# In the last 24 groups of a state-space scan, one u*B product moves from VectorE to GpSimd and its decay to PSUM

## The chip, the cores and the metric

The kernel runs on one core of a Trainium2 chip. The metric is the device time of one execution in microseconds (us); lower is better. Before the change the median of three runs is 1768.24 us (1761.63 to 1771.18).

## What is computed

The input x has 8 batches of 512 tokens with 128 channels. It is normalized, and goes through two branches whose results are multiplied and added to x: a selective state-space layer (Mamba), and a mixture of experts with a silu behind it. The 24 groups that the change touches do the first, cut here to what matters:

```
u, dt, B, C       from projections and a short convolution; 256 inner channels, 64 states, 512 tokens a batch
dA                = exp(dt[t, d] * A[d, s])                       # the decay
state[t, d, s]    = state[t-1, d, s] * dA[t, d, s] + (dt*x)[t, d] * B[t, s]
y[t, d]           = sum over s of state[t, d, s] * C[t, s]
out               = x + (x + (y + D*x_ssm) * silu(z) @ Wout) * silu(experts(x))
```

For each state s and each channel there is a recurrence over 512 tokens. Its three inputs are the decay, u*B (u is dt*x), and, for the output, C.

## The kernel before

**Tiling.** The 256 inner channels are two halves (h = 0, 1) of 128 partitions; the 512 tokens of a batch lie along the free axis. One scan instruction (VectorE, tensor_tensor_scan, 128x512) does one state of one half. The 64 states of a batch are 8 groups of 8 (SG = 8). Over 8 batches there are 64 groups, u = 0 to 63. Groups 0 to 39 carry along the routed experts' matrix work ("with blocks"); groups 40 to 63 (batches 5 to 7) don't, and instead gather the experts' rows and finish the output of batch after batch. The last group of each batch is followed by one that opens the next (40, 48, 56), with extra matrix work and extra VectorE operations (gate_y, add_xn).

**Who does what in a group**, for states i = 0 to 7:

- ScalarE makes the decays: exp with the state's A as scale, from dt_in to `decay` in SBUF (group_decay, L962 to L966). It runs one group ahead: the slot of (i, h) is free when the scan of (i, h) of the group before is done. It also makes diagonals of B (group_diag) and the gelu of the shared expert, once a group.
- u*B is made in one of several ways, by the letter of the state in `KIND` (L64). "D": the matrix unit (PE) broadcasts the row of B to a PSUM bank (bcast, L1462), and VectorE multiplies it twice, by u of each half (L1250), into two PSUM banks. "E": PE makes u*B itself with the diagonal of B (fill, L1473), a half at a time. "Q": the broadcast and one multiplication for the first half; for the second half GpSimd multiplies u by a row of B that a DMA has broadcast to SBUF (L724, into `u_q`), and its decay is written to the PSUM bank by ScalarE (q_decay_to_psum, L948). "P": both halves by GpSimd, both decays to PSUM. Before the change the groups without blocks are "DEDDEDEE", those with blocks "DEDDEQEP".
- VectorE scans: 16 scans a group into `states[:, i % 2]`, a buffer of two states. State i waits for the product of state i - 2 (L1252).
- GpSimd multiplies the finished state by C, both halves in one operation of 128x1024 (L710), once both scans are done. Without blocks it also issues three gathers a group, behind products 1, 4 and 7 (GATHER_AT, L692), 64 in all, so that groups 40 to 60 have all three and group 61 one; and in seven groups gate_attn (L701) behind product 7.
- PE adds the products up to y in PSUM (ysum, add_to_y, L1498), with products in a ring of four.
- SyncE issues the loads of each group (load_group, L464): half of the rows of C at a time, broadcast to all partitions (1024 KB). The first half for group u waits for products 0 to 3 of group u - 1, the second half for all products of group u - 1.

Order on each engine is the order of the program; each works through its own list and waits on semaphores. GpSimd's list for a group is:

```
for i in range(SG):
    (at i = 0 and 4: wait for the rows of C)
    wait scans of state i; product i                     # L708 to L713
    if blocks and i == 1:         u_b                    # L718
    if blocks and i == Q_AT - 2:  u_q                    # L724, Q_AT = 5
    if not blocks: gather at i = 1, 4, 7; gate_attn at i = 7
```

The three PSUM banks that rotate through the states are given by `BANKS`, which is worked out from KIND. States of kinds D and Q leave VectorE's product in the bank that held the state before.

Of the kernel before, what the change touches and what calls it, by code (L numbers as in the profile page):

```python
# [10 lines left out]
ACT = mybir.ActivationFunctionType  # L11
X_AXIS = mybir.AxisListType.X
ds = bass.ds

P = 128
# [4 lines left out]
def mamba_gated_moe(nc, x, norm_w, norm_b, Win, conv_w, conv_b, dt_w, dt_b, A_log, Dskip, Bp, Cp, Wout,  # L20
# [42 lines left out]

    KIND = ("DEDDEDEE", "DEDDEQEP")  # L64
    P_AT, Q_AT = SG - 1, KIND[1].index("Q")
    assert KIND[1].index("P") == P_AT and not set("PQ") & set(KIND[0])
    D_AT = [[i for i in range(SG) if kind[i] == "D"] for kind in KIND]
# [13 lines left out]
    col_of_b = lambda g, e: g if e == NE[1] else g * NE[1] + (E + e)  # L81
    DECAYS = (SCANS, SCANS - NH - 1)
    BROADCASTS = [sum(k in "DQ" for k in kind) for kind in KIND]
# [27 lines left out]
    with ctx:  # L111
# [195 lines left out]
        def _(sp):  # L307
# [147 lines left out]

            def load_b_row(u, g, tb):
                if not isinstance(u, int) or u:
                    sp.wait_ge(s["u_b_pooled"], u)
                    sp.wait_ge(s["u_q_pooled"], u)
                for n in range(2):  # L460
                    sp.dma_start(b_row[:, n, :], c_d[S + n * E:S + (n + 1) * E][ds(g, 1), ds(tb, L)].broadcast_to((P, L))
                                 ).then_inc(s["b_row_loaded"], 16)

            def load_group(b, g, block, block_before):  # L464
# [15 lines left out]
                if isinstance(u, int) and u == ADD_IN[-1] + 1:  # L480
                    sp.wait_ge(s["final_summed"], NB - 1)
                    load_gates(NB - 1)
                if block:
                    load_b_row(u, g, tb)
                load_c(b, g, 1, tb)
# [145 lines left out]
        def _(pool):  # L631
# [71 lines left out]
            def group(b, g, blocks, slot=None, slot_q=None):  # L703
                n = b * S + g * SG
                for i in range(SG):
# [8 lines left out]
                    if blocks and i == 1:  # L714
# [6 lines left out]
                            b_row[:, 0:1, :].broadcast_to((P, NH, L)), ALU.mult).then_inc(s["u_b_pooled"], 1)  # L721
                    if blocks and i == Q_AT - 2:

                        nc.gpsimd.tensor_tensor(u_q, u_in.rearrange("p n h t -> p (n h t)")[:, ds(slot_q, L)], b_row[:, 1, :],  # L724
                                                ALU.mult).then_inc(s["u_q_pooled"], 1)
# [19 lines left out]
        def _(act):  # L745
# [202 lines left out]
            def q_decay_to_psum(u, g, slot):  # L948

                act.sem_inc(s["q_bank_claimed"], 1)  # L950
                col = snap(g * SG + (S + Q_AT))
                nc.scalar.activation(ps[BANKS[True][Q_AT][1]][:], dflat[:, ds(slot + L, L)], ACT.Exp,
                                     scale=aflat[:, ds(col, 1)]).then_inc(s["q_decay_ready"], 1)
# [21 lines left out]
            def group(b, g, slot, head, block, block_before, last=None):  # L975
# [6 lines left out]
                for i in range(SG):  # L982
# [16 lines left out]
                    for h in range(NH):  # L999
                        if block_before and not second and (i, h) == (Q_AT - 1, 1):  # L1000
                            evict_block(u - 1)
                        act.wait_ge(s["scanned"], m0 + (2 * i + h + 1))
                        if block_before and (i, h) in ((P_AT - 2, 1), (P_AT - 1, 0)):
                            decay_to_psum(*before, 1 - h)
                        if block_before and (i, h) == (Q_AT - 1, 0):
                            q_decay_to_psum(*before)
                        if KIND[block][i] == "P" or (KIND[block][i] == "Q" and h) or (first and i == 0):
                            continue
                        group_decay(b, g, slot, i, h)
# [33 lines left out]
            for b in range(NB_BLK, NB):  # L1043
                run(b, False, b == NB_BLK)
            silu_of(NB - 1, ffn_ps[:])
            copy_result(NB - 1, hid_ps)
# [3 lines left out]
        def _(dve):  # L1050
# [182 lines left out]
            def group(b, g, slot, block, last=None, last_xn=None):  # L1233
# [3 lines left out]
                for i in range(SG):  # L1237
# [15 lines left out]
                    for h, bank in enumerate((first, second)):  # L1253
# [7 lines left out]
                        if KIND[block][i] == "Q" and h:  # L1261
# [5 lines left out]
                        dve.wait_ge(s["decay_ready"],  # L1267
                                    states_to(u, DECAYS, block, m + (0 if block and i > Q_AT else 1)))
                        if KIND[block][i] in "DQ":
# [458 lines left out]
```

## Time and profile before

| | |
|---|---|
| median of three runs | 1768.24 us |
| the profiled execution | 1764.14 us |
| its span | 1762.4 us, 43563 instructions |
| VectorE (DVE) busy | 1602.0 us, 91% |
| PE busy | 1549.5 us, 88% |
| GpSimd (POOL) busy | 1487.3 us, 84% |
| ScalarE (ACT) busy | 1402.0 us, 80% |
| the 24 groups without blocks | from 1159.4 to 1748.7 us |

The profile is of one execution. Busy shares are means over the whole span: they tell who is close to full, not who is waited for. Of use here are the timelines of single engines, in which each entry has its start, its length, the line and the operation; "xN" are N operations in a row, merged. In square brackets is the idle time of the engine ahead of the entry and what ended it.

### The profile page before, as it was taken

The numbers are of one execution on the slowest core, as the hardware profiler recorded it, in microseconds if no ns is written. First come the engines' busy times: TensorE is split into PE (matmuls) and PEld (weight loads), VectorE is DVE, ScalarE is ACT, GpSimd is POOL, SyncE is SP. The second block draws the span as 40 slices with busy tenths as digits, with TensorE's granted clock in tenths as the row PEclk, the third lists the DMA queues.
The fourth block names the chain that finished last, engine by engine and source line by source line (L and its number), as shares of the span: only waits on it lengthen the run. The fifth ranks groups of instructions, "written<-read, shape, count | busy, mean of one in ns | idle before, by whom it ended". The sixth has DMA issues, their size and how long they took to land. (4 is left out here: it accounts for less than half of the span.)

```text
span 1762.4 us, 43563 instructions
## 1 busy us (share of the span) xinstructions
PE 1549.5 (88%) x13334; PEld 799.8 (45%) x13334; DVE 1602.0 (91%) x1778; ACT 1402.0 (80%) x2641; POOL 1487.3 (84%) x757
## 2 busy tenths in 40 slices
PE   5784489999999999999999999988898988999888
PEld 5332254444444544444444444444443444444444
DVE  7888489999999999999999999999998999999987
ACT  4898478887888888887888788888888788888882
POOL 1355489998999999999999899989998899989976
PEclk8897699999999999999999999999999999999999
DMA  8767555676676875686667757666456464664633
GB/s 237 248 221 228 144 134 147 150 175 173 151 161 145 200 159 145 151 203 165 150 149 172 181 151 159 148 150 141 115 120 170 111 135 99 151 138 107 141 81 80
DMA packets 215321, 272.45 MB, mean 155 GB/s; under 512 B 27530, under 2 KB 106132, under 8 KB 215060
## 3 DMA queue, kind: packets, MB, share of 16 engines
q1 hardware_dynamic: 211124, 262.66, 61.6%
q0 software_dynamic: 4096, 8.40, 1.7%
q8 instruction: 69, 1.13, 0.3%
q14 instruction: 32, 0.26, 0.0%
HBM read 226.81 MB, written 43.93 MB: 154 GB/s over the span
## 5 line engine op out<-in xcount | busy, mean ns | idle before, releaser
L710 POOL TENSOR_TENSOR arena<-arena 128x1024 f32<-128x1024 f32 x512 | 1199.8, 2360 | 138.7 <-DVE arena L1275 114.6
L1275 DVE TENSOR_TENSOR_SCAN arena<-arena,ps 128x512 f32<-128x512 f32 x904 | 1045.2, 1204 | 91.3 <-POOL arena L710 57.2
L965 ACT ACTIVATE arena<-arena,neg_A 128x512 f32<-128x512 f32 (+1 forms) x904 | 605.5, 712 | 76.7 <-DVE arena L1275 73.9
L1498 PE MATMUL ps<-arena,ident 64*64 64x512 f32 x4096 | 557.0, 616 | 1.7 <-POOL arena L710 1.6
L1484 PE MATMUL ps<-arena 128*64 128x128 f32 x6912 | 469.4, 280 | 99.8 <-DVE arena L1275 96.9
L1484 PEld LDWEIGHTS ps<-arena 128*64 128x64 f32 x6912 | 374.1, 138 | 331.2 <-DVE arena L1275 179.7
L1250 DVE TENSOR_TENSOR ps<-arena,ps 128x512 f32<-128x512 f32 x472 | 301.3, 680 | 9.5 <-PE ps L1470 9.4
L972 ACT ACTIVATE arena<-ident,b_turned 128x128 f32<-128x128 f32 x864 | 272.9, 387 | 0.0
L1498 PEld LDWEIGHTS ps<-arena,ident 64*64 64x64 f32 x4096 | 107.6, 131 | 180.6 <-issue 173.7
L925 ACT ACTIVATE arena<-ps,arena 128x256 f32<-128x256 f32 x160 | 67.0, 470 | 118.8 <-PE ps L1568 118.8
L682 POOL DMA_INDIRECT x_rms_by_expert<-arena,slots x64 | 70.4, 1099 | 96.4 <-DMA x_rms_by_expert<-arena,slots 61.3
L1470 PEld LDWEIGHTS ps<-b_parts,pick 96*128 96x128 bf16 (+1 forms) x256 | 24.6, 96 | 249.3 <-issue 212.2
L1470 PE MATMUL ps<-b_parts,pick 96*128 96x512 bf16 x256 | 100.8, 394 | 40.2 <-DVE arena L1275 33.8
L718 POOL TENSOR_TENSOR arena<-arena 128x1024 f32<-128x1024 f32 x40 | 94.8, 2369 | 0.0
L1258 DVE TENSOR_TENSOR_SCAN arena<-ps,arena 128x512 f32<-128x512 f32 x80 | 93.1, 1205 | 0.2 <-POOL arena L710 0.2
L917 ACT ACT_TABLE_LOAD x64 | 82.1, 1283 | 13.9 <-PE ps L1547 9.2
L965 ACT ACT_TABLE_LOAD x70 | 89.8, 1283 | 1.2
L1576 PE MATMUL ps<-arena 128*128 128x128 f32 x640 | 89.8, 285 | 0.0
L1576 PEld LDWEIGHTS ps<-arena 128*128 128x128 f32 x640 | 82.7, 196 | 11.1 <-issue 10.0
L1568 PE MATMUL ps<-arena 128*128 128x256 f32 x320 | 86.5, 393 | 0.0
L1547 PE MATMUL ps<-x_rms,arena 128*128 128x512 f32 x128 | 67.9, 612 | 5.2 <-issue 4.5
L692 POOL DMA_INDIRECT arena<-routed_by_expert,slots x64 | 63.2, 987 | 9.5 <-issue 3.7
(171 smaller groups left out, 1138.2 us busy)
## 6 DMA issues: line engine op xcount, KB each, us to landing
arena<-c_scratch SPq DMA_DIRECT2D x128, 1024.0 KB
arena<-c_scratch SPq DMA_DIRECT2D x80, 256.0 KB, 6.4
arena<-w_routed_scaled SPq DMA_DIRECT2D x40, 256.0 KB
arena<-in_L_ffn_W_r_dram SPq DMA_DIRECT2D x40, 256.0 KB, 9.1
arena<-w_shared_tiles SPq DMA_DIRECT2D x128, 64.0 KB
x_rms_by_expert<-arena SPq DMA_DIRECT2D x1, 5120.0 KB, 28.1
arena<-x_rms_by_expert SPq DMA_DIRECT2D x40, 128.0 KB, 7.3
routed_by_expert<-arena SPq DMA_DIRECT2D x40, 128.0 KB, 8.8
```

The source lines that it names most:

```text
L710: nc.gpsimd.tensor_tensor(products[:, i % RING, :, :], states[:, i % 2, :, :], c_rows[:, i // CG, i % CG, :].unsqueeze(1).broadcast_to((P, ...
L718: nc.gpsimd.tensor_tensor(u_b, u_in.rearrange("p n h t -> p (n h t)")[:, ds(slot, NH * L)].rearrange("p (h t) -> p h t", h=NH), b_row[:, 0 ...
L965: nc.scalar.activation(decay[:, 2 * i + h, :], dflat[:, ds(slot + h * L, L)], ACT.Exp, scale=aflat[:, ds(col, 1)]).then_inc(s["decay_ready ...
L972: ins = nc.scalar.activation(diag_of(e)[:, c, :], ident[:], ACT.Copy, scale=bt_flat[:, ds(at + c, 1)])
L1250: vector.tensor_tensor(ps[bank][:], uflat[:, ds(slot + h * L, L)], ps[new][:], ALU.mult).then_inc(s["u_b_multiplied"], 1)
L1258: vector.tensor_tensor_scan(states[:, i % 2, h, :], ps[bank][:], u_b[:, h, :], 0.0, ALU.mult, ALU.add).then_inc(s["scanned"], 1)
L1275: vector.tensor_tensor_scan(states[:, i % 2, h, :], decay[:, m, :], ps[bank][:], 0.0, ALU.mult, ALU.add).then_inc(s["scanned"], 1)
L1470: mm(ps[bank][:], pick[:, ds(sel, 1)].broadcast_to((3 * SQ, P)), bflat[:, ds(col, L)], start=True, stop=True).then_inc(s["b_broadcast"], 1)
L1484: ins = mm(bank[HP * r:HP * r + HP, c * P:(c + 1) * P], u_turned[:, odd, c, h * P + HP * r:h * P + HP * r + HP], diag[:, c, :], start=True ...
L1498: ins = mm(y_ps[r][HP * h:HP * h + HP, :], ident[q, q], products[q, slot, h, :], start=False, stop=False, skip_group_check=True)
L1568: mm(bank[:, (RA, RB)[t % 2]], w1_block[:, t, :], x_block, start=True, stop=True, skip_group_check=True).then_inc(s["tile_made"], 1)
L1576: ins = mm(block_ps[:, k * C:(k + 1) * C], hidden_block[:, t, k * P:(k + 1) * P], w2_block[:, t, :], start=(t == 0), stop=(t == HT - 1), s ...
```

## The change

The kind of state 5 (the sixth) in the groups without blocks goes from D to Q. VectorE multiplies only for the first half of the channels; GpSimd makes u*B of the second half to SBUF, behind product 3; ScalarE writes the decay of the second half to the PSUM bank instead of to `decay` in SBUF, in the group in which it is read, not one ahead; SyncE loads the row of B for it (256 KB) once a group, which so far it did only with blocks. The plan of PSUM banks for these groups becomes that of the groups with blocks. For group 63 ScalarE writes its decay behind its last group.

```diff
-    KIND = ("DEDDEDEE", "DEDDEQEP")
+    KIND = ("DEDDEQEE", "DEDDEQEP")
...
-    DECAYS = (SCANS, SCANS - NH - 1)
+    DECAYS = (SCANS - 1, SCANS - NH - 1)
...
-            def load_b_row(u, g, tb):
+            def load_b_row(u, g, tb, block=True):
                 if not isinstance(u, int) or u:
-                    sp.wait_ge(s["u_b_pooled"], u)
+                    if block:
+                        sp.wait_ge(s["u_b_pooled"], u)
                     sp.wait_ge(s["u_q_pooled"], u)
-                for n in range(2):
+                for n in range(0 if block else 1, 2):
...
-                if block:
-                    load_b_row(u, g, tb)
+                load_b_row(u, g, tb, block)
                 load_c(b, g, 1, tb)
...
-                    if blocks and i == Q_AT - 2:
+                    if i == Q_AT - 2:
+                        if not blocks:
+                            pool.wait_ge(s["b_row_loaded"], (b * E + g) * 16 + (NBLK * 16 + 16))
+                            pool.wait_ge(s["dt_u_loaded"], b * 32 + 32)
+                            slot_q = (b % 2) * (NH * L) + L
                         nc.gpsimd.tensor_tensor(u_q, u_in.rearrange("p n h t -> p (n h t)")[:, ds(slot_q, L)], b_row[:, 1, :],
                                                 ALU.mult).then_inc(s["u_q_pooled"], 1)
...
-                        if block_before and (i, h) == (Q_AT - 1, 0):
+                        if not first and (i, h) == (Q_AT - 1, 0):
                             q_decay_to_psum(*before)
...
+            act.wait_ge(s["scanned"], NB * E * SCANS + 2 * (Q_AT - 1) + 1)
+            q_decay_to_psum(NB * E - 1, E - 1, (NB - 1) % 2 * (NH * L))
```

The rest of the diff carries the same through the counts of semaphores and asserts.

## Rows read from the trace of the kernel before

**Rows 1.** Costliest lines, 1160 to 1750 us; then busy time by engine in one group.

```profile
L1275 DVE TENSOR_TENSOR_SCAN arena<-arena,ps 128x512 f32<-128x512 f32 x384 | 441.4, 1202 | 27.4 <-POOL arena L710 14.1 <-PE ps L1484 8.3 <-ACT arena L965 3.2
...
core 0: us, PE busy (x) PEld busy (x) DVE busy (x) ACT busy (x) POOL busy (x), PEclk, DMA share, GB/s
...
1303.50:1326.90 23.40, 21.80 (x222) 11.57 (x224) 22.71 (x25) 20.59 (x37) 21.64 (x11) 1.00 0.57 105
```

**Rows 2.** Timeline of VectorE, group 46: start, length, line, operation, [idle before].

```profile
1313.75 4.54 DVE L1275 TENSOR_TENSOR_SCAN arena<-arena,ps 128x512 f32<-128x512 f32 x4
1318.22 1.26 DVE L1250 TENSOR_TENSOR ps<-arena,ps 128x512 f32<-128x512 f32 x2
1319.39 4.54 DVE L1275 TENSOR_TENSOR_SCAN arena<-arena,ps 128x512 f32<-128x512 f32 x4
1324.63 2.33 DVE L1275 TENSOR_TENSOR_SCAN arena<-arena,ps 128x512 f32<-128x512 f32 x2 [0.69 <-POOL arena L710]
1326.88 1.27 DVE L1250 TENSOR_TENSOR ps<-arena,ps 128x512 f32<-128x512 f32 x2
```

**Rows 3.** Timeline of GpSimd, the same group.

```profile
1316.22 4.67 POOL L710 TENSOR_TENSOR arena<-arena 128x1024 f32<-128x1024 f32 x2 [0.84 <-DVE arena L1275]
1321.04 0.99 POOL L692 DMA_INDIRECT arena<-routed_by_expert,slots  x1
1322.05 4.68 POOL L710 TENSOR_TENSOR arena<-arena 128x1024 f32<-128x1024 f32 x2
1327.10 2.36 POOL L710 TENSOR_TENSOR arena<-arena 128x1024 f32<-128x1024 f32 x1 [0.37 <-DVE arena L1275]
```

**Rows 4.** Timelines, group 38 (with blocks, state 5 a Q); then all of L724.

```profile
1127.66 0.67 DVE L1250 TENSOR_TENSOR ps<-arena,ps 128x512 f32<-128x512 f32 x1
1128.37 1.22 DVE L1275 TENSOR_TENSOR_SCAN arena<-arena,ps 128x512 f32<-128x512 f32 x1
...
1131.30 2.33 DVE L1275 TENSOR_TENSOR_SCAN arena<-arena,ps 128x512 f32<-128x512 f32 x2 [0.59 <-POOL arena L710]
...
1127.48 1.29 POOL L724 TENSOR_TENSOR arena<-arena 128x512 f32<-128x512 f32 x1
1128.72 4.68 POOL L710 TENSOR_TENSOR arena<-arena 128x1024 f32<-128x1024 f32 x2
...
L724 POOL TENSOR_TENSOR arena<-arena x40: 1259/1278/1297, 203.7 to 1151.1; 128x512 f32<-128x512 f32 x40
```

**Rows 5.** Timelines of GpSimd and VectorE, group 63 (no gathers).

```profile
1738.18 4.67 POOL L710 TENSOR_TENSOR arena<-arena 128x1024 f32<-128x1024 f32 x2 [1.06 <-DVE arena L1275]
1743.82 4.66 POOL L710 TENSOR_TENSOR arena<-arena 128x1024 f32<-128x1024 f32 x2 [0.96 <-DVE arena L1275]
...
1746.38 2.33 DVE L1275 TENSOR_TENSOR_SCAN arena<-arena,ps 128x512 f32<-128x512 f32 x2 [0.48 <-POOL arena L710]
```

**Rows 6.** Timelines: waits for others in groups 41, 43, 48, 49, 57, 62.

```profile
1184.50 1.29 DVE L1250 TENSOR_TENSOR ps<-arena,ps 128x512 f32<-128x512 f32 x2 [0.42 <-PE ps L1470]
...
1232.04 1.29 DVE L1250 TENSOR_TENSOR ps<-arena,ps 128x512 f32<-128x512 f32 x2 [0.21 <-PE ps L1470]
...
1360.30 2.33 DVE L1275 TENSOR_TENSOR_SCAN arena<-arena,ps 128x512 f32<-128x512 f32 x2 [5.69 <-PE ps L1484]
...
1384.07 1.29 DVE L1250 TENSOR_TENSOR ps<-arena,ps 128x512 f32<-128x512 f32 x2 [1.08 <-PE ps L1470]
...
1577.88 1.30 DVE L1250 TENSOR_TENSOR ps<-arena,ps 128x512 f32<-128x512 f32 x2 [0.75 <-PE ps L1470]
...
1689.17 1.28 ACT L933 ACTIVATE arena<-ident,gate_columns 128x128 f32<-128x128 f32 x4 [4.83 <-PE ps L1517]
...
1711.35 1.29 DVE L1250 TENSOR_TENSOR ps<-arena,ps 128x512 f32<-128x512 f32 x2 [4.74 <-PE ps L1470]
```

**Rows 7.** ScalarE's decays (to PSUM; to SBUF at state 4); landing times of L461.

```profile
L952 ACT ACTIVATE ps<-arena,neg_A x40: 666/692/693, 218.7 to 1150.9; 128x512 f32 x32, 128x512 f32<-128x512 f32 x8
...
1222.00 0.72 ACT L965 ACTIVATE arena<-arena,neg_A 128x512 f32<-128x512 f32 x1 [0.39 <-DVE arena L1275]
...
DMA to landing us min/median/max: 3.8/6.4/10.8
```

More of the change, by code:

```diff
@@ L58, in mamba_gated_moe @@
     N_SUM = SG
-    KIND = ("DEDDEDEE", "DEDDEQEP")
+    KIND = ("DEDDEQEE", "DEDDEQEP")
     P_AT, Q_AT = SG - 1, KIND[1].index("Q")
-    assert KIND[1].index("P") == P_AT and not set("PQ") & set(KIND[0])
+    assert KIND[1].index("P") == P_AT and "P" not in KIND[0] and KIND[0].index("Q") == Q_AT
     D_AT = [[i for i in range(SG) if kind[i] == "D"] for kind in KIND]
@@ L951, in q_decay_to_psum @@
                 col = snap(g * SG + (S + Q_AT))
-                nc.scalar.activation(ps[BANKS[True][Q_AT][1]][:], dflat[:, ds(slot + L, L)], ACT.Exp,
+                nc.scalar.activation(ps[BANKS[0][Q_AT][1]][:], dflat[:, ds(slot + L, L)], ACT.Exp,
                                      scale=aflat[:, ds(col, 1)]).then_inc(s["q_decay_ready"], 1)
@@ L1267, in group @@
                         dve.wait_ge(s["decay_ready"],
-                                    states_to(u, DECAYS, block, m + (0 if block and i > Q_AT else 1)))
+                                    states_to(u, DECAYS, block, m + (0 if i > Q_AT else 1)))
                         if KIND[block][i] in "DQ":
```

## Prediction

> **What bounds the kernel now.** I read the lines of the stretch without blocks (1160 to 1750 us) first. The scans of VectorE (L1275) had 27.4 us of idle time ahead of them, and half of it, 14.1 us, ended with a product of GpSimd (L710) [rows 1]. So VectorE is nearly full, and what it does wait for most is GpSimd. One ordinary group shows the same: of 23.40 us VectorE is busy for 22.71 and GpSimd for 21.64 [rows 1]. A removed VectorE operation is therefore worth its time only where GpSimd isn't the next to be late, and that has to be read in order of time.
>
> I take group 46 (states counted 0 to 7; VectorE's in rows 2, GpSimd's in rows 3). Scans of states 3 and 4 start at 1313.75, two per state, 1.12 us apart (four in 4.55 us); the two multiplications of state 5 follow at 1318.22, the scans of states 5 and 6 at 1319.39, and then VectorE idles for 0.69 us and starts state 7 at 1324.63 [rows 2]. GpSimd starts the product of state 3 at 1316.22, when the scans of state 3 are done, and from there never idles: products 3 and 4, a gather at 1321.04, products 5 and 6 at 1322.05 [rows 3]. Product 5 ends about 1324.4, and 0.24 us later state 7 starts, since it writes the buffer that product 5 reads. So the **bound of the group** from state 3 to state 7 is a chain on GpSimd: product 3, product 4, gather, product 5. VectorE alone would have been there 0.69 us earlier. After state 7 the two are together again: product 7 starts at 1327.10 after 0.37 us of idling [rows 3], and what follows is set by VectorE up to state 3, where GpSimd has idled 0.84 us.
>
> **The change, part by part.** *VectorE loses one multiplication a group.* Two take 1.17 us from their start to the first scan (1318.22 to 1319.39) [rows 2]; a single one ahead of such a scan takes 0.71 (1127.66 to 1128.37, a group with blocks) [rows 4]. That is 0.46 us a group; by half of the pair's 1.17 it would be 0.59. For 24 groups the ends are 11.0 and 14.2 us. This time lies between state 4 and state 6, that is beside the chain on GpSimd: it makes the wait longer, not the group shorter.
>
> *GpSimd gains one product of 128x512 a group.* In the groups with blocks it takes 1.24 us from its start to that of the next (1127.48 to 1128.72) [rows 4]. It is put behind product 3 (i = Q_AT - 2), inside the chain. Product 4 then starts at 1316.22 + 2.34 + 1.24 = 1319.80 and ends at 1322.16; state 6 can't start before 1322.40, where VectorE alone would have it at 1319.39 - 0.46 + 2.24 = 1321.17, so a new wait of 1.2 us appears there. The groups with blocks show its like: behind the same operation, state 6 waits 0.59 us for GpSimd [rows 4]. The gather starts at about 1322.3, product 5 at 1323.29, and state 7 at 1324.63 + 1.24 = 1325.87. VectorE has state 6 done at 1324.64, so state 7 waits another 1.2 us. Product 7 finds GpSimd free (product 6 ends 1.24 later too, and so does the scan before it), and the next group starts **1.24 us later** than now. Nothing of it is given back by the 0.84 us of idling, which lies ahead of product 3.
>
> A rule of the Trainium skill bears on this ("Perfetto Trace Analysis", Optimizing Scalar/DVE Operations): VectorE and GpSimd share an SBUF read port, so moving operations from one to the other might not help. The 40 operations of this kind took 1259 to 1297 ns beside a busy VectorE [rows 4], so what the trace shows is no blocking at the port; by the rule alone, with the operation blocked for a scan, a group would lose 1.12 us more.
>
> *By kind of group.* The full 1.24 us holds where a gather stands behind product 4 and state 7 waits for GpSimd: groups 40 to 60 but for these. Group 47 is followed by a stall of 5.69 us ahead of state 1 of group 48, which the matrix unit ends [rows 6]; it hangs on transfers that are issued earlier, at state 4 of group 47, and swallows the loss: 0. In groups 48 and 56, which open a batch, the first multiplication behind them waits for the matrix unit for 1.08 and 0.75 us anyway [rows 6], so of 1.24 at most 0.2 and 0.5 are left: I take 0.4 in all. In group 40 that wait is 0.42 [rows 6]: 0.8 left. In 42, 45, 51, 54, 57 and 60 it is about 0.21 (group 42 is shown) [rows 6]: 1.03 each, 6.2. The other eleven (41, 43, 44, 46, 49, 50, 52, 53, 55, 58, 59) give 11 x 1.24 = 13.6. Group 61 is followed by a stall of 4.74 us in group 62; ScalarE's work behind a wait of 4.83 us ends it [rows 6], with its count of operations unchanged: 0. Groups 62 and 63 have no gather. There, state 7 starts at 1746.38, that is 8.35 us after the end of state 3's scans (1738.03, 0.15 ahead of product 3) [rows 5]. With the new operation it can't start before 0.15 + 2.34 + 1.24 + 2.34 + 2.34 + 0.24 = 8.65: 0.3 each, 0.6 in all. The sum is 13.6 + 6.2 + 0.8 + 0.4 + 0.6 = **21.6 us**.
>
> *ScalarE* writes one decay a group to PSUM in place of one to SBUF: 0.69 against 0.72 us [rows 7], nothing. But it now writes it for the group that VectorE is in, behind the wait for the first scan of state 4. At that step it stands in line with VectorE (0.39 us idle for it) [rows 7]. In group 46 the scan ends about 1317.2, the decay would be written by 1318.1, and it is read at about 1318.22 + 0.71 + 1.12 = 1320.0: 1.9 us of cover. Behind the wait are queued only decays of the next group. Group 61 lacks that cover (the 4.83 us wait is just ahead), and may lose up to 2 us, inside its stall. If the cover failed everywhere, the wait would be hidden up to 1.2 us by the wait at state 6.
>
> *SyncE* gets a wait and a broadcast of 256 KB a group, ahead of its second C load. Such a load lands in 3.8 to 10.8 us [rows 7]; it is issued behind product 3 of the group before, and read a group (23 us) later. The C load behind it waits for product 7, a longer wait. Cost 0, and about 1 us if it crowds a late C load once. PE's broadcasts are the same in number. The other order of PSUM banks costs nothing that the rows show; bound 0.1 us a group either way.
>
> **Rivals.** *VectorE sets the pace after all*: the new operation fits into GpSimd's idle time (23.40 - 21.64 = 1.76 a group) and 24 x 0.46 to 0.59 are saved: 11 to 14 us faster, 1757 us. It needs the idle time to lie inside the chain; it lies ahead of products 3 and 7 [rows 3]. It decides if state 7 no longer waits. Chance 0.07. *Partly hidden*: the gather doesn't hold up product 5 in full, and groups lose 0.3 as those without gather: 24 x 0.3 = 7 us slower, 1775 us. The gather's place in the row of starts (1321.04, 1322.05) speaks against it. Chance 0.10. *More than one thing late*: the wait at state 6 puts the matrix unit or the late decay behind as well, 0.5 us more a group: 21.6 + 12 = 34 us, 1801 us. For it speaks that 8.3 us of VectorE's waits are for fills [rows 1]; against it, that all of them get more time. Chance 0.05. The forecast has 0.78. That the edit changes other groups than the 24 is ruled out by its text.
>
> **How the numbers follow.** The profiled execution took 1764.14 us (span 1762.4, 1.7 around it), 4.1 below the median of the three runs, 1768.24. 1764.1 + 21.6 = 1785.7; by the median 1789.8. I put the time at 1788 us, 1.2% slower than before. The range runs from the partly hidden case, 1775, to 1800, just short of the worst; 1 in 10 is left out at each side. Under 0.5% (9 us) this kernel's runs can't be told from no change: they spread over 9.5 us. So slower by more than that 0.78 + 0.05 = 0.83, within it 0.10, faster 0.07.
>
> **What would show it.** In the profile after: multiplications on L1250 down by 24, 24 more of GpSimd's 128x512 and of the decays to PSUM; in an ordinary group a period of about 24.8 us, VectorE idle ahead of states 6 and 7 by 1.2 us each with GpSimd as what ended it, and no idle time on GpSimd from product 3 to 6. VectorE's waits for GpSimd in the stretch go from 14 to 50 us. The forecast is wrong if state 7 starts without a wait, if the stalls at 48 and 62 stay as long as they are (then 2.5 us more), or if the first wait is for the decay in PSUM.

## The result, and the profile after

The changed kernel takes 1785.81 us (median of 8 runs, 1779.12 to 1791.45); beside it on the same chip the kernel before takes 1768.65 us (median of 8). The ratio is 1.0098, with a 95% interval from 1.0080 to 1.0117. The forecast was 1788 us and 1.2% slower; it is 1.0% slower, by 17 us. The profiled execution took 1784.35 us with a span of 1782.5 us, against 1764.14 and 1762.4 before.

The page's row of engines for the kernel after, and its rows for the multiplications and for GpSimd's new operation:

```profile
PE 1552.5 (87%) x13334; PEld 802.6 (45%) x13334; DVE 1593.8 (89%) x1754; ACT 1403.9 (79%) x2642; POOL 1515.2 (85%) x781
...
L1257 DVE TENSOR_TENSOR ps<-arena,ps 128x512 f32<-128x512 f32 x448 | 286.8, 679 | 6.3 <-PE ps L1477 6.3
...
L729 POOL TENSOR_TENSOR arena<-arena 128x512 f32<-128x512 f32 x64 | 82.0, 1281 | 0.0
```

VectorE has 24 operations fewer and is busy for 8.2 us less (1602.0 before); GpSimd has 24 more and is busy for 27.9 us more (1487.3 before). The busiest engine has less to do, and the kernel is slower. Next, where the scans wait (costliest line from 1160 to 1770 us, the counterpart of [rows 1]), then group 46 as a window, then two of VectorE's waits in the same stretch as the first row (who waits for whom: total, times, longest):

```profile
L1282 DVE TENSOR_TENSOR_SCAN arena<-arena,ps 128x512 f32<-128x512 f32 x360 | 416.9, 1205 | 55.6 <-POOL arena L711 36.9 <-ACT arena L970 10.4 <-PE ps L1491 5.7
...
core 0: us, PE busy (x) PEld busy (x) DVE busy (x) ACT busy (x) POOL busy (x), PEclk, DMA share, GB/s
...
1311.90:1336.60 24.70, 21.75 (x224) 11.42 (x216) 22.34 (x25) 21.68 (x38) 22.99 (x12) 1.00 0.50 111
...
DVE arena L1282 <- ACT arena L970: 10.4, 13, 1.1
...
DVE arena L1271 <- ACT ps L957: 1.4, 1, 1.4
```

The scans' idle time has doubled, from 27.4 to 55.6 us, and what ends it is GpSimd: 36.9 us by name. The 10.4 us put down to L970 of ScalarE are GpSimd's too. A scan there waits for several semaphores, and the profile names only one of them. In all 13 cases a product of GpSimd, the one that reads the scan's buffer, ends 0.21 us ahead of the scan's start, as it does at the waits that are put down to GpSimd. With them it is about 47 us.

Group 46 after the change, VectorE's timeline (start, length, line, operation, idle before it), the counterpart of [rows 2]:

```profile
1322.21 4.54 DVE L1282 TENSOR_TENSOR_SCAN arena<-arena,ps 128x512 f32<-128x512 f32 x4
1326.68 0.67 DVE L1257 TENSOR_TENSOR ps<-arena,ps 128x512 f32<-128x512 f32 x1
1327.38 1.22 DVE L1282 TENSOR_TENSOR_SCAN arena<-arena,ps 128x512 f32<-128x512 f32 x1
1328.52 1.20 DVE L1271 TENSOR_TENSOR_SCAN arena<-ps,arena 128x512 f32<-128x512 f32 x1
1330.81 2.33 DVE L1282 TENSOR_TENSOR_SCAN arena<-arena,ps 128x512 f32<-128x512 f32 x2 [1.09 <-POOL arena L711]
1334.34 2.33 DVE L1282 TENSOR_TENSOR_SCAN arena<-arena,ps 128x512 f32<-128x512 f32 x2 [1.20 <-POOL arena L711]
1336.59 1.27 DVE L1257 TENSOR_TENSOR ps<-arena,ps 128x512 f32<-128x512 f32 x2
1337.89 4.55 DVE L1282 TENSOR_TENSOR_SCAN arena<-arena,ps 128x512 f32<-128x512 f32 x4
```

And GpSimd's, the counterpart of [rows 3]:

```profile
1324.68 2.38 POOL L711 TENSOR_TENSOR arena<-arena 128x1024 f32<-128x1024 f32 x1 [0.84 <-DVE arena L1282]
1327.00 1.29 POOL L729 TENSOR_TENSOR arena<-arena 128x512 f32<-128x512 f32 x1
1328.23 2.37 POOL L711 TENSOR_TENSOR arena<-arena 128x1024 f32<-128x1024 f32 x1
1330.74 0.99 POOL L693 DMA_INDIRECT arena<-routed_by_expert,slots  x1
1331.75 4.69 POOL L711 TENSOR_TENSOR arena<-arena 128x1024 f32<-128x1024 f32 x2
1336.82 2.36 POOL L711 TENSOR_TENSOR arena<-arena 128x1024 f32<-128x1024 f32 x1 [0.38 <-DVE arena L1282]
```

The two can be laid over the rows of before. From the start of the scans of states 3 and 4 to the start of state 7 it was 1324.63 - 1313.75 = 10.88 us and is 1334.34 - 1322.21 = 12.13 us: 1.25 more. GpSimd runs from product 3 to product 6 without idling, and waits ahead of product 3 for 0.84 us as before. In place of one wait of 0.69 us there are two, of 1.09 ahead of state 6 and 1.20 ahead of state 7.

Four more rows of VectorE's timeline answer to [rows 6]: the stall in group 48, the wait behind it, the scan that reads the decay in PSUM in group 61, and the stall in group 62:

```profile
1368.57 2.33 DVE L1282 TENSOR_TENSOR_SCAN arena<-arena,ps 128x512 f32<-128x512 f32 x2 [3.01 <-PE ps L1491]
...
1392.35 1.29 DVE L1257 TENSOR_TENSOR ps<-arena,ps 128x512 f32<-128x512 f32 x2 [1.07 <-PE ps L1477]
...
1712.29 1.22 DVE L1271 TENSOR_TENSOR_SCAN arena<-ps,arena 128x512 f32<-128x512 f32 x1 [1.43 <-ACT ps L957]
...
1730.87 1.29 DVE L1257 TENSOR_TENSOR ps<-arena,ps 128x512 f32<-128x512 f32 x2 [3.12 <-PE ps L1477]
```

From the first scan of one group's state 0 to that of the next, both timelines give the length of every group. Those marked gate_attn are the ones in which GpSimd also does gate_attn's operation (L702, 1.24 us), which is issued behind product 7 of the group before and so falls into their time; 47, 56 and 62 have it as well.

| groups | before | after | each | sum | forecast |
|---|---|---|---|---|---|
| 40 | 25.11 | 25.94 | +0.83 | +0.8 | +0.8 |
| 43, 46, 52, 55, 58 | 23.35 to 23.38 | 24.72 to 24.76 | +1.34 to +1.41 | } | } |
| 44, 50, 53, 59 (with gate_attn) | 24.22 to 24.25 | 25.32 to 25.37 | +1.09 to +1.14 | } +13.6 | } +13.6 |
| 41, 49 | 23.68 | 24.74, 24.93 | +1.06, +1.25 | } | } |
| 42, 45, 51, 54, 57, 60 | 23.86 (51: 24.31, 57: 24.93) | 24.73 (57: 25.68) | +0.43 to +0.88 | +4.7 | +6.2 |
| 47 and 48 | 24.24, 32.98 | 25.34, 30.45 | +1.10, -2.53 | -1.4 | 0 (+0.4 with 56) |
| 56 | 26.78 | 26.71 | -0.07 | -0.1 | (with 48) |
| 61 and 62 | 23.16, 28.02 | 24.38, 26.77 | +1.22, -1.25 | 0.0 | +0.3 |
| 63 | 22.06 | 22.30 | +0.24 | +0.2 | +0.3 |
| first scan of 40 to last of 63 | 588.1 | 606.0 | | +17.8 | +21.6 |

The span grew by 20.1 us. The 2.3 us that the table doesn't hold lie ahead of group 40, where the two kernels do the same work; the first scan of group 40 starts anywhere from 1158.5 to 1165.7 us in the ten profiles of this document, and the medians differ by 17.2 us, which agrees with the table. So the 2.3 is taken for scatter and not for an effect of the change.

### The profile page after: what moved, and what is told of

Read it like the earlier page. It is cut to its first block, busy times and chain, and to the rows that moved or that the text cites. A ratio compares the mean times of both kernels' runs of the same rounds, so it can differ in the third digit from the quotient of the medians.

```text
span 1782.5 us, 43612 instructions
## 1 busy us (share of the span) xinstructions
PE 1552.5 (87%) x13334; PEld 802.6 (45%) x13334; DVE 1593.8 (89%) x1754; ACT 1403.9 (79%) x2642; POOL 1515.2 (85%) x781
## 4 chain that ended last, share of the span: by engine, by line
issue 28%; POOL 23%; DMA 21%; PE 11%; ACT 8%; DVE 6%; SPq 1%; POOLq 1%; DVEq 0%; ACTq 0%
POOL arena L711 18%; DMA arena<-c_scratch 15%; DMA x_rms_by_expert<-arena,slots 6%; ACT arena L970 4%; DVE arena L1282 4%; PE ps L1491 3%; PE ps L1505 3%; ACT arena L977 2%; POOL arena L719 2%; POOL x_rms_by_expert L683 1%; POOL arena L729 1%; DVE ps L1257 1%; SPq L334 1%; ACT L970 1%; POOL arena L693 1%
## 5 line engine op out<-in xcount | busy, mean ns | idle before, releaser
L1282 DVE TENSOR_TENSOR_SCAN arena<-arena,ps 128x512 f32<-128x512 f32 x880 | 1020.7, 1205 | 121.6 <-POOL arena L711 82.0
L970 ACT ACTIVATE arena<-arena,neg_A 128x512 f32<-128x512 f32 (+1 forms) x880 | 589.1, 713 | 88.4 <-DVE arena L1282 77.0
L1257 DVE TENSOR_TENSOR ps<-arena,ps 128x512 f32<-128x512 f32 x448 | 286.8, 679 | 6.3 <-PE ps L1477 6.3
L1265 DVE TENSOR_TENSOR_SCAN arena<-ps,arena 128x512 f32<-128x512 f32 x80 | 93.0, 1205 | 0.2 <-POOL arena L711 0.2
L1271 DVE TENSOR_TENSOR_SCAN arena<-ps,arena 128x512 f32<-128x512 f32 x64 | 76.7, 1199 | 14.1 <-ACT ps L957 14.1
L729 POOL TENSOR_TENSOR arena<-arena 128x512 f32<-128x512 f32 x64 | 82.0, 1281 | 0.0
```

The costliest lines, as they stand in the source:

```text
L970: nc.scalar.activation(decay[:, 2 * i + h, :], dflat[:, ds(slot + h * L, L)], ACT.Exp, scale=aflat[:, ds(col, 1)]).then_inc(s["decay_ready ...
L1257: vector.tensor_tensor(ps[bank][:], uflat[:, ds(slot + h * L, L)], ps[new][:], ALU.mult).then_inc(s["u_b_multiplied"], 1)
L1265: vector.tensor_tensor_scan(states[:, i % 2, h, :], ps[bank][:], u_b[:, h, :], 0.0, ALU.mult, ALU.add).then_inc(s["scanned"], 1)
L1282: vector.tensor_tensor_scan(states[:, i % 2, h, :], decay[:, m, :], ps[bank][:], 0.0, ALU.mult, ALU.add).then_inc(s["scanned"], 1)
```

## The experiments

**The theory** is that of the forecast: GpSimd's operation lies in the chain product 3, product 4, gather, product 5, and costs its own 1.24 us there. **Rivals**: the time comes from somewhere else in the change (ScalarE's decay to PSUM and its waits, or the banks' order); it is the shared port and not the chain; or it is GpSimd's whole load and not the place. Each ratio is to the kernel before, measured beside it on the same chip. "Ordinary" is a group like 43 and 46, without gate_attn and without a wait for the matrix unit; "of kind 42" are 42, 45, 51, 54, 57 and 60, behind which the kernel before waits for the matrix unit.

### Everything but GpSimd's operation

```diff
+                        if not blocks:
+                            pool.sem_inc(s["u_q_pooled"], 1)
+                        else:
                             nc.gpsimd.tensor_tensor(u_q, ...
```

> The changed kernel with everything it adds (the wait and load of SyncE, the decay to PSUM by ScalarE, the second bank plan, one multiplication less) but without GpSimd's 128x512 operation in the 24 groups, so that state 5 of the second half of the channels is computed from stale u*B there. Theory (the operation lies in GpSimd's chain product 3, product 4, gather, product 5): the chain is that of before, state 7 starts 8.56 us after the scans of state 3, VectorE waits 0.7 us plus the 0.46 that it saves; the period of an ordinary group is 23.4 to 23.5 us, in all 0 to 3 us over before, ratio 1.000 to 1.002. Rival (the loss comes from the decay to PSUM, the loads or the bank plan): stays near the changed kernel, ratio 1.007 to 1.010.

Measured: 1764.8 us, ratio 0.9981 [0.9966, 0.9997], a little below the 1.000 to 1.002 that was expected. An ordinary group takes 23.50 us, the 24 groups together ("the stretch") 589.7. VectorE's timeline in group 46 of this kernel:

```profile
1319.92 2.31 DVE L1285 TENSOR_TENSOR_SCAN arena<-arena,ps 128x512 f32<-128x512 f32 x2
1323.38 2.33 DVE L1285 TENSOR_TENSOR_SCAN arena<-arena,ps 128x512 f32<-128x512 f32 x2 [1.16 <-POOL arena L711]
```

State 6 doesn't wait. State 7 waits for GpSimd for 1.16 us, where it waited 0.69 before: the 0.46 us that VectorE saves are there, and they are wait. So the saving without the price is worth 0.2% at most, not the 11 to 14 us of VectorE's own account, and the profile shows no gain in the stretch, which is 1.6 us longer than before: ordinary groups are 0.14 longer, most of those of kind 42 0.33 shorter (23.53 in place of 23.86), as their wait for the matrix unit is gone. What lies between this kernel and the changed one comes from the one operation: 16.3 us by the stretches (606.0 - 589.7), about 21 us by the ratios (0.9981 to 1.0098).

### The operation alone, in the kernel before

```diff
-                    if blocks and i == Q_AT - 2:
+                    if i == Q_AT - 2:
+                        if not blocks:
+                            slot_q = (b % 2) * (NH * L) + L
+                            pool.wait_ge(s["dt_u_loaded"], b * 32 + 32)
```

> The kernel before with nothing but GpSimd's 128x512 operation added behind product 3 in the last 24 groups; nobody reads its result. Theory: 1.24 us more in an ordinary group (period 24.6), state 6 and state 7 wait for GpSimd, 14 to 17 us in all, ratio 1.008 to 1.0095; that VectorE keeps its multiplication changes nothing. Rival (the operation fits into GpSimd's 1.76 us of idle time, and the loss comes from elsewhere): ratio 1.000 to 1.002.

Measured: 1788.03 us, ratio 1.0104 [1.0065, 1.0143], somewhat above the 1.008 to 1.0095 that was expected, which the interval includes; an ordinary group takes 24.60 us, 1.24 more than before. States 6 and 7 in VectorE's timeline:

```profile
1332.46 2.33 DVE L1278 TENSOR_TENSOR_SCAN arena<-arena,ps 128x512 f32<-128x512 f32 x2 [0.62 <-POOL arena L710]
1335.99 2.33 DVE L1278 TENSOR_TENSOR_SCAN arena<-arena,ps 128x512 f32<-128x512 f32 x2 [1.19 <-POOL arena L710]
```

This kernel keeps VectorE's multiplication, and it loses as much as the changed one. The wait ahead of state 6 is 0.62 here and 1.09 after: the difference, 0.47, is what the removed multiplication is worth, and it turns up as wait. Both halves agree: within the intervals, GpSimd's operation is the whole of the loss, with or without the rest of the change. Whether it is its place or its mere length is for the next kernel.

### The operation one product earlier

```diff
-                    if i == Q_AT - 2:
+                    if i == (Q_AT - 2 if blocks else Q_AT - 3):
```

> The changed kernel with GpSimd's new operation behind product 2 instead of product 3 in the 24 groups, where 0.83 us of idle time lies just behind it (0.26 in the groups that follow gate_attn). Theory: product 3 starts 0.41 us late (1.0 in those groups), so an ordinary group has a period of 23.9 us in place of 24.74, and the whole is 8 to 11 us over before, ratio 1.0045 to 1.0065. Rival (the operation costs its length wherever it stands, or the cost isn't its place): ratio 1.009 to 1.010.

Measured: 1774.09 us, ratio 1.0031 [1.0013, 1.0049]. GpSimd's timeline from product 2 to product 4 in group 46, then VectorE's wait ahead of state 7 in the same group (the profile names ScalarE, but here too a product of GpSimd, product 5, ends 0.21 us ahead of the scan):

```profile
1321.05 2.37 POOL L711 TENSOR_TENSOR arena<-arena 128x1024 f32<-128x1024 f32 x1
1323.36 1.29 POOL L729 TENSOR_TENSOR arena<-arena 128x512 f32<-128x512 f32 x1
1324.60 4.68 POOL L711 TENSOR_TENSOR arena<-arena 128x1024 f32<-128x1024 f32 x2
...
1333.03 2.33 DVE L1282 TENSOR_TENSOR_SCAN arena<-arena,ps 128x512 f32<-128x512 f32 x2 [1.21 <-ACT arena L970]
```

The same operation with the same load, behind product 2: it fills the 0.84 us of idling that lay ahead of product 3, and an ordinary group takes 23.87 us in place of 24.74. The 1.21 us ahead of state 7 stay, as the gather is still in the chain; the 1.09 that the operation had made ahead of state 6 are gone, and 0.25 ahead of state 5 have come in their place. So it is the place, and not the load alone, that makes up two thirds of the loss. The rest remains because the idle time (0.84) is shorter than the operation (1.24). Groups with gate_attn take 25.03, since there GpSimd is late from product 0 on. The total came out a little below what was expected.

### The decay in SBUF

Here the decay of the Q half is written to SBUF, as in the kernel before, and the scan reads both inputs from there. It tests the rival of the port. ScalarE's order and the counts of semaphores, not shown, follow it.

```diff
-    DECAYS = (SCANS - 1, SCANS - NH - 1)
+    DECAYS = (SCANS, SCANS - NH - 1)
...
-                            vector.tensor_tensor_scan(states[:, i % 2, h, :], ps[bank][:], u_q, ...
+                            vector.tensor_tensor_scan(states[:, i % 2, h, :], ps[bank][:] if block else decay[:, m, :], u_q, ...
```

> The changed kernel with the decay of state 5, second half, written by ScalarE to SBUF one group ahead, as before the change; VectorE's scan there then has both inputs in SBUF. Theory as it stands (the decay is not on the chain): as the changed kernel, ratio 1.009 to 1.011, the scan and GpSimd's product beside it at 1.20 and 2.36 us. Rival by the page SBUF - State Buffer of the Trainium skill (a VectorE operation with two SBUF inputs and a GpSimd operation that reads SBUF shut each other out for their whole length): the product or the scan is held by 1 to 2.4 us a group, which shows as a longer scan, a longer product or a gap, and 24 to 50 us more in all, ratio 1.023 to 1.04.

Measured: 1801.49 us, ratio 1.0186 [1.0152, 1.0221]. The theory's figure was missed. The rival's mechanism is there, though at a lower price than it was given. Timelines of VectorE and GpSimd in an ordinary group, and all scans of L1270 by form (count, then min/median/max in ns, and from when to when):

```profile
1307.44 3.15 DVE L1270 TENSOR_TENSOR_SCAN arena<-arena 128x512 f32<-128x512 f32 x1
...
1307.14 2.36 POOL L711 TENSOR_TENSOR arena<-arena 128x1024 f32<-128x1024 f32 x1
1309.65 1.73 POOL L693 DMA_INDIRECT arena<-routed_by_expert,slots  x1 [0.15 <-issue]
1311.40 4.67 POOL L711 TENSOR_TENSOR arena<-arena 128x1024 f32<-128x1024 f32 x2
...
L1270 DVE TENSOR_TENSOR_SCAN arena<-ps,arena x40: 1196/1197/1223, 218.5 to 1155.3; 128x512 f32<-128x512 f32 x40
L1270 DVE TENSOR_TENSOR_SCAN arena<-arena x24: 2181/3148/3167, 1180.0 to 1779.0; 128x512 f32<-128x512 f32 x24
```

The scan takes 3.15 us, not 1.20. It starts at 1307.44, just after product 4 has started, and ends at 1310.59, which is 1.09 us after product 4 ends (1309.50), about its usual length: it behaves as if it ran only once GpSimd was done. The delay comes back to GpSimd: the gather behind product 4, which starts while the scan is still open, takes 1.73 us in place of 0.99 (21 of the 64 gathers are that long, none in the other kernel), and from the start of product 4 to that of product 5 it is 4.26 us, against 3.52 after the change. That is the 0.73 us by which an ordinary group is longer (25.47 against 24.74). In the changed kernel, with the decay in PSUM, none of this shows: its 64 scans of that kind take 1.20 us on average. The Trainium skill states it so ("SBUF — State Buffer", Who interferes with whom): a VectorE instruction with two inputs in SBUF contends with a GpSimd instruction that reads SBUF, by an exclusive lock, and one with at most one SBUF input, outside its two-port modes, does not. The scans here agree with both halves.

### The gather one product later

```diff
-    GATHER_AT = (1, 4, 7)
+    GATHER_AT = (1, 5, 7)
```

> The changed kernel with the second gather of a group behind product 5 instead of product 4. Theory: the gather's 1.16 us leaves the chain between product 3 and product 5, but then stands ahead of product 6, and GpSimd has no idle time left: product 7 starts 0.8 us later against state 7 than now, state 2 of the next group waits for product 0. The period goes from 24.74 to about 23.7 us, near GpSimd's own sum of 8 x 2.34 + 1.24 + 3 x 1.16 = 23.4; ratio 1.000 to 1.003. Rival (the chain isn't what sets the group; the place of the gather is without effect): ratio 1.009 to 1.010.

Measured: 1774.08 us, ratio 1.0046 [1.0031, 1.0062]. VectorE's timeline, the scans of states 6 and 7 of one group, then those of state 2 in the next, which has gate_attn (the 1.25 us are put down to ScalarE, but product 0 ends 0.2 us ahead of the scan):

```profile
1326.78 4.65 DVE L1282 TENSOR_TENSOR_SCAN arena<-arena,ps 128x512 f32<-128x512 f32 x4 [0.90 <-POOL arena L711]
...
1339.71 2.33 DVE L1282 TENSOR_TENSOR_SCAN arena<-arena,ps 128x512 f32<-128x512 f32 x2 [1.25 <-ACT arena L970]
```

An ordinary group takes 23.54 us (23.7 was expected): with the gather out of the chain, its 1.2 us are back. But the four groups with gate_attn take 24.93 to 25.46, 3.9 us in all over the kernel before, as now GpSimd ends its list later, product 0 of the next group starts later, and state 2 waits 1.25 us. The total is above what was expected in part for that reason: the stretch is 9.4 us longer than before, and groups 40, 45, 48 and 56 hold another 4.6, which no run explains.

### The gather one earlier, without the change

The kernel before, with the gather taken out of the chain into GpSimd's idle time.

```diff
-    GATHER_AT = (1, 4, 7)
+    GATHER_AT = (1, 2, 7)
```

> The kernel before with the second gather behind product 2 instead of product 4, nothing else. Theory: product 3 starts 0.3 us late (0.9 in the groups behind gate_attn), product 4 ends in time all the same, product 5 starts right behind the scans of state 5, and state 7 starts 8.35 us after the scans of state 3 in place of 8.56: period 23.2 in place of 23.4, 3 to 5 us in all, ratio 0.9970 to 0.9985. Rival (the 0.69 us ahead of state 7 is the round trip scan, product, scan alone, or what is won is lost at the stalls of groups 48 and 62): ratio 0.999 to 1.001.

Measured: 1767.99 us, ratio 0.9999 [0.9988, 1.0009]. Timelines of GpSimd (products 5 and 6) and VectorE (state 7) in group 46 of this kernel:

```profile
1326.19 4.68 POOL L710 TENSOR_TENSOR arena<-arena 128x1024 f32<-128x1024 f32 x2 [0.63 <-DVE arena L1275]
...
1328.76 2.33 DVE L1275 TENSOR_TENSOR_SCAN arena<-arena,ps 128x512 f32<-128x512 f32 x2 [0.49 <-ACT arena L965]
```

With the gather out of the way product 5 waits for the scans of state 5, and state 7 still waits 0.49 us (product 5 ends 0.21 us ahead of it). So of the 0.69 us of the kernel before only 0.20 are the gather's; the other 0.49 is the round trip from the scans of state 5 over product 5 to state 7, which is left when the gather is gone. The chain on GpSimd was the bound of the group before, but only by 0.20 us. Ordinary groups are 0.20 us shorter (23.16), as expected, but the groups of kind 42 and those with gate_attn gain nothing: the matrix unit or product 0 is late there. The stretch is 1.5 us shorter in the profile, which the medians can't tell from no change. The expected gain was missed.

### Both moves in the changed kernel

```diff
-    GATHER_AT = (1, 4, 7)
+    GATHER_AT = (1, 5, 7)
...
-                    if i == Q_AT - 2:
+                    if i == (Q_AT - 2 if blocks else Q_AT - 3):
```

> The changed kernel with both moves: GpSimd's operation behind product 2, the second gather behind product 5. The chain from state 3 to state 7 then holds three products alone and could be 7.9 us. Theory (GpSimd's own sum of 23.4 us a group is the floor of any order with this operation): period 23.4 to 23.5 us, GpSimd without idle time but 0.1 us, no gain over the kernel before in groups with gathers; ratio 0.998 to 1.001. Rival (VectorE sets the pace once the chain is short: 22.0 us of its own operations and 0.13): period 22.5 to 22.8 us, 14 to 20 us faster than before, ratio 0.989 to 0.992.

Measured: 1774.8 us, ratio 1.0046 [1.0032, 1.0061], above the 0.998 to 1.001 that was expected. The waits at state 7 and in a group with gate_attn, from VectorE's timeline, then product 5 of the same group 46 on GpSimd:

```profile
1325.99 2.33 DVE L1282 TENSOR_TENSOR_SCAN arena<-arena,ps 128x512 f32<-128x512 f32 x2 [0.40 <-POOL arena L711]
...
1336.60 2.33 DVE L1282 TENSOR_TENSOR_SCAN arena<-arena,ps 128x512 f32<-128x512 f32 x2 [1.25 <-POOL arena L711]
...
1323.41 2.37 POOL L711 TENSOR_TENSOR arena<-arena 128x1024 f32<-128x1024 f32 x1 [0.36 <-DVE arena L1271]
```

The three kinds of group (ordinary, 42, with gate_attn) take 23.12, 24.52 and 25.05 us, 24.2 on average, where the kernel before takes 23.8. Now it is GpSimd's sum that counts: 8 products at 2.34, the new one at 1.24, three gathers' places at 1.16, together 23.44 us, and with gate_attn's 1.24 in every third group 23.85. To this comes the one place where GpSimd still idles, 0.36 us a group ahead of product 5, whose scans had to wait for product 3: 24.2 us, which is the average measured. VectorE's own sum is below that (22.34 us busy in group 46 after), and the rival by which VectorE would set a pace of 22.5 to 22.8 is gone. The expectation had left gate_attn and this wait out of GpSimd's sum.

### The banks' order alone

The kernel before, with the plan of PSUM banks that the changed kernel has in the groups without blocks.

```diff
+    BANKS[0] = bank_plan(set(range(SG)) - set(D_AT[0]) | {0, 5})
```

> The kernel before with another plan of PSUM banks: in states 0 and 5 the bank of the broadcast is the one that is scanned first, as the changed kernel has it in state 0. Theory: its scan then waits for the multiplication just ahead of it, 1.30 us from the start of the pair to the first scan in place of 1.17; in state 0 the 0.13 us is on VectorE's path, in state 5 it is covered by the wait at state 7: 24 x 0.13 = 3 us, ratio 1.001 to 1.002, period 23.5 us. Rival (the 0.13 us in state 0 of the changed kernel has another cause, such as the longer wait ahead of it): 1.17 us in both places and ratio 1.000.

Measured: 1773.8 us, ratio 1.0041 [1.0026, 1.0056]. VectorE's timeline, group 46 of this kernel:

```profile
1320.95 1.26 DVE L1252 TENSOR_TENSOR ps<-arena,ps 128x512 f32<-128x512 f32 x2
1322.25 4.55 DVE L1277 TENSOR_TENSOR_SCAN arena<-arena,ps 128x512 f32<-128x512 f32 x4
1327.36 2.33 DVE L1277 TENSOR_TENSOR_SCAN arena<-arena,ps 128x512 f32<-128x512 f32 x2 [0.56 <-POOL arena L712]
1329.61 1.27 DVE L1252 TENSOR_TENSOR ps<-arena,ps 128x512 f32<-128x512 f32 x2
1330.91 4.55 DVE L1277 TENSOR_TENSOR_SCAN arena<-arena,ps 128x512 f32<-128x512 f32 x4
```

From the start of a pair of multiplications to the first scan it is 1.30 us here (1320.95 to 1322.25, and 1329.61 to 1330.91), where [rows 2] have 1.17. In this plan the first scan reads the bank that the second multiplication has just written; in the other, the one before it. Ahead of state 5 the 0.13 us is covered by the wait at state 7 (0.56 in place of 0.69); ahead of state 0 it is not. An ordinary group takes 23.50 us, 0.13 more, as expected, and one of kind 42 takes 0.26 more. The stretch is 5.1 us longer in the profile, the medians differ by 5.6 and the ratio stands for 7 us, where 3 had been expected. In the profile groups 40, 48 and 53 hold 3.2 of the 5.1 us; whether the bank order does that isn't settled. In the kernel without GpSimd's operation, which has this plan too, the stretch is only 1.6 us longer than before.

## Why the prediction was right, and where it was off

**What bounds a group: right.** The chain on GpSimd from product 3 to state 7 was the theory, and the operation and the gather were each moved by themselves. The operation in the chain costs an ordinary group 1.24 us with or without the rest of the change (23.36 to 24.60, 23.50 to 24.74); without it nothing is lost; behind product 2 most of the loss goes; with the gather out of the chain the ordinary group is back at 23.54. What the forecast didn't say is how little the chain was ahead: 0.20 us of the 0.69 (the gather one earlier). The rest of the wait is the round trip over product 5. The signs that it named are there: period 24.74 (24.8 forecast), waits of 1.09 and 1.20 us (1.2 each forecast), no idle time from product 3 to product 6, VectorE's waits for GpSimd at about 47 us (50 forecast).

**VectorE's saved multiplication: right in place, nothing in worth.** 0.46 us was taken for it; the wait at state 7 without GpSimd's operation is 0.47 longer than before (1.16 to 0.69), and the wait at state 6 with it is 0.47 longer than with the multiplication kept (1.09 to 0.62).

**The eleven ordinary groups: the sum is right, and by two errors that cancel.** 13.6 was forecast, 13.6 measured. The five of kind 43 lost 1.34 to 1.41, that is 1.24 and 0.13 for the banks' order. The forecast said of this order that it "costs nothing that the rows show", with a bound of 0.1 us a group; it costs 0.13, over the bound. Its [rows 2] are of a group without blocks. The groups with blocks already have the Q and the banks that go with it, and there the trace of the kernel before shows the price, at state 0 (VectorE's timeline):

```profile
1135.79 1.27 DVE L1250 TENSOR_TENSOR ps<-arena,ps 128x512 f32<-128x512 f32 x2
1137.09 4.55 DVE L1275 TENSOR_TENSOR_SCAN arena<-arena,ps 128x512 f32<-128x512 f32 x4
```

These are 1.30 us from the pair's start to the scan, against 1.17 in [rows 2]; it could have been read. The four with gate_attn and group 41 lost 1.06 to 1.14, less than 1.24. With gate_attn, product 0 was late in the kernel before too, and state 2 waits 0.64 us before and 0.51 after: there the 0.13 of the banks' order is covered. The last 0.14 is in GpSimd's timeline of such a group, 44: products 3 and 4 before the change, then product 3 and the operation in the kernel with the operation alone.

```profile
1268.87 4.80 POOL L710 TENSOR_TENSOR arena<-arena 128x1024 f32<-128x1024 f32 x2 [0.27 <-DVE arena L1275]
...
1277.16 2.36 POOL L710 TENSOR_TENSOR arena<-arena 128x1024 f32<-128x1024 f32 x1 [0.26 <-DVE arena L1278]
1279.49 1.28 POOL L727 TENSOR_TENSOR arena<-arena 128x512 f32<-128x512 f32 x1
```

The pair takes 4.80 us, against 4.67 in group 46 [rows 3]: the scans of state 4 are late there, and product 4 has a hole of 0.13 us ahead of it. The operation starts in that hole, 2.33 us after product 3, and so adds only 1.11. Group 41 had 0.32 us of its own before (23.68 against 23.36) that is gone after.

**The six groups with a wait for the matrix unit: mis-sized.** The term was 1.03 each, 6.2, and is 4.7. The wait of 0.21 was taken off, and it is only a part of what the late matrix unit costs such a group. VectorE's timeline, state 7 of group 42 before (the pair behind it is the 0.21 of [rows 6]), and the same place after:

```profile
1229.33 2.50 DVE L1275 TENSOR_TENSOR_SCAN arena<-arena,ps 128x512 f32<-128x512 f32 x2 [0.70 <-POOL arena L710]
...
1234.74 2.33 DVE L1282 TENSOR_TENSOR_SCAN arena<-arena,ps 128x512 f32<-128x512 f32 x2 [1.19 <-POOL arena L711]
1236.99 1.27 DVE L1257 TENSOR_TENSOR ps<-arena,ps 128x512 f32<-128x512 f32 x2
```

From the start of state 7 to that of the pair it was 2.71 us before and is 2.25 after: the second scan was late as well (2.50 in place of 2.33). In all a group of kind 42 took 23.86 us before, 0.50 more than an ordinary one, and takes 24.73 after, no more than an ordinary one. So the cover was 0.50 and not 0.21, and with the 0.13 of the banks' order 1.24 + 0.13 - 0.50 = 0.87 is left, which is what four of the six lost (0.86 to 0.88). Group 51 lost only 0.43, since it had 0.45 us of irregular time before that is gone after; 57 (0.75) has such time in both.

**The stalls at 48 and 62: swallowed, and more.** The forecast took groups 47 and 61 at zero, each giving its delay to the stall behind it. Groups 61 and 62 did so to 0.03 us (+1.22, -1.25), but by another delay than the one that the forecast fed in: group 61 has no gather behind product 4, with the operation alone it takes 23.40 us (+0.24), and with everything but the operation 24.36 (+1.20). What makes it longer is ScalarE's late decay (below). In 47 and 48 it is +1.10 and -2.53, and the stall went from 5.69 to 3.01 us, by 2.7, more than the 1.24 it was fed. Group 48 takes from 30.5 to 34.2 us over the profiles of the ten kernels with no order in it that follows their edits, so the surplus of 1.4 may be scatter; this stays open. Without it the 24 groups would have lost 19.2 us, 2.4 below the forecast. The 0.4 for 48 and 56 isn't seen: 56 is level, and the wait behind it had covered the whole.

**ScalarE's decay to PSUM: right.** It has its cover everywhere but in group 61, where the scan waits 1.43 us for it (up to 2 were forecast; the kernel without GpSimd's operation has the same 1.43), and the stall in group 62 is shorter by that and more (3.12 in place of 4.74). What the forecast didn't see is what the decay's place in PSUM does for the change: without it the loss would be nearly twice as large (1.0186). The forecast weighed the port rule on GpSimd's operation, where the rows showed no blocking, and that held; it didn't weigh it on the scan that reads what that operation wrote.

**SyncE and transfers: nothing seen.** GpSimd's new operation has no idle time ahead of it, so no load of B rows was late, and GpSimd's waits for rows of C come to 3.3 us in the stretch, against 5.6 before.

**The sum.** 21.6 us was forecast, the table gives 17.8 and the medians 17.2. The four terms that were too high are the six groups (1.5), 47 and 48 (1.4 and the 0.4 with 56), 61 and 62 (0.3) and 63 (0.1). That the sum laid on the profiled execution, 1785.7 us, is the measured median to 0.1 us is luck: the median of before was 4 us above its profile, and the sum was 4 us too high. The forecast of 1788 was set between that and 1789.8. The rivals fall by the runs: VectorE doesn't set the pace, even with all of the operation's cost out of the chain; the gather does hold up product 5 (moved behind it, 1.20 us a group come back); and nothing else came late but the decay in group 61.

## What to carry to other kernels

Work that is moved from the busiest engine to the next one is paid by its place in the second engine's row, not by the busy shares: read in order of time which operations of the second engine stand between two steps of the first, and put the new one where that engine idles. If the idle stretch there is shorter than the operation, the rest is still paid, and if its whole list is as long as the period, the list is the next bound: here 23.85 us of GpSimd's work against a period of 23.8. When both work on SBUF together, look at whether the busy engine's instruction reads two operands there; one of them in PSUM was worth 0.73 us a group.

## What the runs showed of the hardware

A VectorE scan of 128x512 that has both inputs in SBUF takes 3.15 us beside a GpSimd product of 128x1024 (median of 24); in an ordinary group it starts 0.30 us behind the product and ends 1.09 us after it; with one input in PSUM the same scan takes 1.20 us (64 cases). A gather that started 0.94 us before such a scan ended took 1.73 us in place of 0.99, and ended 0.79 us after it.

A gather takes GpSimd 0.99 us and 1.16 us of its row, a product of 128x512 1.24 us and one of 128x1024 2.34 us from start to start.

A VectorE scan that reads the PSUM bank that the multiplication right ahead of it wrote starts 0.13 us later than one with an operation between the two (1.30 against 1.17 us from the pair's start).
